# Router shares carried in the routed rows, and routed sums added by accumulating DMAs, in a two-layer kernel

## Chip, core and metric

The kernel runs on one core of a Trainium2 chip. The metric is the time of one execution on the device in microseconds. The core has TensorE (PE), VectorE (DVE), ScalarE (ACT), GpSimd (POOL) and SyncE (SP), each with an instruction stream of its own that runs strictly in order; they wait for each other by semaphores. SP issues plain DMAs, POOL the indirect ones (gathers and scatters by a list of row numbers).

## What is computed

Sixteen sequences of 256 tokens, 256 dimensions, go through two layers. The part that matters here is the mixture of experts of layer 0 and what layer 1 does first:

```python
x = x + tanh(g_xattn[0]) * retention(layernorm(x), ctx, ctx)
# router: 32 experts, the best 6 of a token, their scores normed to a sum of 2.5
topk_w = topk_w / (topk_w.sum(-1, keepdims=True) + 1e-20) * ROUTED_SCALE
h = relu2(einsum('th,eih->tei', x, up_w)) * combine[:, :, None]
moe_out = einsum('tei,ehi->th', h, down_w)
x = x + tanh(g_ffn[0]) * (moe_out + shared_expert(x))
# layer 1
x = x + tanh(g_xattn[1]) * softmax_attention(layernorm(x), ctx, ctx)   # 16 heads of 16
x = x + tanh(g_ffn[1]) * spiking_ffn(layernorm(x))
```

The share of an expert is a factor of its output row, so it may be applied wherever that row is at hand.

## The kernel before

The 16 sequences are eight groups of two (T = 512 tokens, four blocks `tt` of 128). Three stretches follow one another.

**Layer 0** (0 to about 511 us). Each engine has a list of steps with slot numbers; `turns` (L470) merges the steps of up to four groups into turns of 36 slots, older groups first within a slot. In it DVE works out for each group: the token's norm, the low half of the row (`low_row`, L835, a row is the token as two 16-bit halves, 1024 bytes), the router (`route_*`, up to L890), the rank of a token at its expert and so its row number (`rank`, `slot`, `slot_row`, L895 to L906), the shares (`weigh`, L911 to L925) and `add_shared` (L935). `weigh` stands at slot 97 of a group, that is slot 25 of a turn. It multiplies the chosen scores by their norm (`combine`, 128 x 4 x 32) and then picks the six shares of a token by comparing row numbers, in three operations of 128x768, into `share`, which stays in SBUF to layer 1. PE transposes the rows (L589) for the router and the shared expert. POOL sends each group's rows to the experts' places in HBM by 24 indirect DMAs (`xs<-w_hi,slot_row`, L1026), when the low halves and the row numbers are there.

**The routed experts** (about 518 to 755 us). 128 tiles of 256 rows in 64 pairs: SP loads a pair of `row_tile` (three buffers), PE transposes it, ACT and DVE copy, PE multiplies by the expert's first weights, ACT and DVE square the positive part, PE multiplies by the second, and two pairs later ACT (L1194) and DVE (L1246) each copy one tile of the output from PSUM, 128x512, to `y_tile`, which SP stores to `ys`. POOL does nothing here.

**Layer 1** (about 760 to 1578 us). Again steps by slots, in turns of 32 (`turns`, L1356), two sequences of 16 slots each to a group. Group g has its front in turn g (moments of x, `rstd`, `xn`, and the projections k, x, q, v by the slots of `FRONT`), its row maxima in the next (L1753), then the exponentials, and the tail (output projection, `power_f` at L1866, spiking network) in the two turns after that. The slots that matter here, in the turn of group g:

- slots 0, 2, 4, 6, 8, 10: DVE's `add_routed(k)` (L1707), four operations of 128x256 each: x_tok = share x y_in + x_tok
- slot 11: `moments_x`; slot 12: POOL's `power_x` (L1862); slot 15: `shift_x`
- slots 1 to 11.75: POOL's 24 gathers of group g+1 into `y_in` (L1856), each k behind the adds of k of group g, which free the buffer
- slots 19, 21, 23, 25: x0, x1, q0, q1 on PE
- slot 8: SP's load of x of group g+1 (L1379), which stands behind copies to `k_stack`
- slots 9 and 25: POOL's `power_f` for the tail of an older group's two sequences; DVE's `shift_f` (L1793) waits for it

The first group's 24 gathers stand ahead of the turns (L1883).

## Time and profile before

| | us |
|---|---|
| median of 3 runs | 1583.79 |
| lowest and highest | 1582.92, 1583.98 |
| the profiled execution | 1580.07 |
| its span from first to last instruction | 1578.3 |
| mean granted TensorE clock of it | 0.815 |

Differences are worked out in the profiled execution, between points of its span, and then set against its own time; that stands 3.7 us below the median, and this difference is added at the end. A row of the timeline gives the start, the duration and, in brackets, how long the engine sat idle before it and what ended that.

### The profile page before, as it was taken

To read this page: it belongs to the slowest core of one execution; us is meant where nothing else is said; L and a number is where in the kernel's file an instruction comes from. 1 tells how busy PE (TensorE), PEld (TensorE's weight loads), DVE (VectorE), ACT (ScalarE), POOL (GpSimd) and SP (SyncE) were. 2 spreads that over 40 slices of the span, in tenths; PEclk is the share of its full clock that TensorE was granted. 3 is DMA by queue.
4 is the path that set the end of the run, shared out by engine and by line. 5 is a ranking of instruction groups with operands and counts; after the bars stand their busy time and mean duration, and the time that the engine had idled before them with its cause. 6 is when DMAs were issued, how large, how long until landed. Compare 5 with 4: busy or idle time off the path is not lost.

```text
span 1578.3 us, 25639 instructions
## 1 busy us (share of the span) xinstructions
PE 1078.2 (68%) x8813; PEld 721.5 (46%) x8813; DVE 964.2 (61%) x2140; ACT 720.2 (46%) x1204; POOL 454.6 (29%) x444
## 2 busy tenths in 40 slices
PE   3766667766642799999204547586887778787875
PEld 1444434544321699899101214353545445454454
DVE  4574464665556477877615557577767767767433
ACT  2332232333343577777101336364646555655552
POOL 1134644653566000000564252406051510000000
PEclk9788878788766899999655659798988979888787
DMA  7513513321222798987534142414142321111100
GB/s 287 193 51 146 187 67 120 133 81 40 81 93 93 235 334 299 313 301 264 177 100 110 51 129 65 128 45 123 39 117 69 112 79 43 42 42 33 42 22 14
DMA packets 108140, 193.42 MB, mean 123 GB/s; under 512 B 21488, under 2 KB 46704, under 8 KB 107504
## 3 DMA queue, kind: packets, MB, share of 16 engines
q1 hardware_dynamic: 89584, 141.44, 27.0%
q0 software_dynamic: 18432, 50.36, 9.9%
q8 instruction: 75, 1.23, 0.3%
q14 instruction: 49, 0.40, 0.1%
HBM read 98.66 MB, written 79.95 MB: 113 GB/s over the span
## 4 chain that ended last, share of the span: by engine, by line
PE 21%; DVE 16%; issue 5%; another core or an unknown queue 4%; ACT 2%; DVEq 2%; DMA 1%; SPq 1%; ACTq 0%
PE bank L357 11%; DVE row_max L1753 5%; PE bank L1561 4%; PE bank L1517 3%; DVE x_tok L1707 3%; DVE spikes L1813 2%; PE bank L1477 2%; DVEq L1705 1%; PE bank L1500 1%; DVE mixed L1771 1%; DVE hid_lo L1804 1%; PE bank L383 1%; DVE spikes L1810 1%; DVE stats L1693 1%
## 5 line engine op out<-in xcount | busy, mean ns | idle before, releaser
L1753 DVE TENSOR_REDUCE row_max<-bank 128x2 f32<-128x512 f32 x256 | 164.9, 684 | 134.2 <-PE bank L1477 82.6
L1026 POOL DMA_INDIRECT xs<-w_hi,slot_row x192 | 196.7, 1024 | 117.6 <-DVE slot_row L906 62.1
L1856 POOL DMA_INDIRECT y_in<-ys,y_row x168 | 172.5, 1027 | 188.5 <-DVE x_tok L1707 141.1
L1625 ACT ACTIVATE prob<-bank 128x512 f32<-128x512 f32 x256 | 138.3, 589 | 90.5 <-PE bank L1500 58.4
L357 PE MATMUL bank<-xf_hi,w_hi 128*128 128x256 f16 (+1 forms) x320 | 114.3, 357 | 36.3 <-DVE xf_lo L1798 28.0
L1477 PE MATMUL bank<-k_stack,q_stack 48*128 48x256 f16 x512 | 58.4, 311 | 100.5 <-DVE row_max L1753 78.7
L357 PE MATMUL bank<-xf_hi,w_lo 128*128 128x256 f16 (+1 forms) x320 | 114.3, 357 | 2.3 <-issue 1.5
L357 PE MATMUL bank<-xf_lo,w_hi 128*128 128x256 f16 (+1 forms) x320 | 115.0, 359 | 1.1 <-issue 1.1
L1866 POOL TENSOR_TENSOR rstd_f<-var_eps_f,minus_half 128x2 f32<-128x2 f32 x16 | 15.0, 937 | 345.8 <-DVE var_eps_f L1698 345.7
L1883 POOL DMA_INDIRECT y_in<-ys,y_row x24 | 23.3, 972 | 256.4 <-issue 256.4
L357 PE MATMUL bank<-xt_tile,w_routed 128*128 128x256 f16 x768 | 95.2, 274 | 0.0
L1707 DVE SCALAR_TENSOR_TENSOR x_tok<-y_in,share,x_tok 128x256 f32<-128x256 f32 x192 | 80.5, 481 | 13.5 <-DMA y_in<-ys,y_row 8.4
L357 PE MATMUL bank<-w_routed,hid_tile_hi 128*128 x512 | 87.3, 273 | 0.8 <-DVE hid_tile_lo L1240 0.8
L357 PE MATMUL bank<-w_hi,ct 128*128 128x256 f16 x256 | 61.1, 323 | 37.6 <-DVE xt_lo L770 35.0
L357 PE MATMUL bank<-ct,w_hi 128*128 128x512 f16 x128 | 48.6, 459 | 54.2 <-DVE ct L794 30.2
L1477 PEld LDWEIGHTS bank<-k_stack,q_stack 48*128 48x128 f16 x512 | 16.4, 97 | 146.4 <-issue 74.6
L1517 PE MATMUL bank<-prob,v_one 128*32 128x256 f32 x1024 | 83.2, 447 | 0.0
L1173 ACT ACTIVATE xt_tile<-bank 128x1024 f16<-128x1024 f16 x64 | 65.5, 1023 | 33.4 <-PE bank L1126 33.4
L1126 PE MATMUL bank<-ident,row_tile 128*128 128x128 f16 x1024 | 69.3, 222 | 15.4 <-DMA row_tile<-xs 12.8
L1561 PE MATMUL bank<-w_hi,hid_hi 128*128 128x256 f16 x256 | 71.9, 281 | 10.0 <-DVE hid_lo L1804 7.1
L1236 DVE TENSOR_TENSOR hid_tile<-relu_tile 128x512 f32<-128x512 f32 x64 | 44.2, 691 | 55.4 <-ACT relu_tile L1183 55.4
L1500 PE MATMUL bank<-q_stack,k_stack 50*128 50x256 f16 x512 | 58.4, 307 | 27.8 <-ACT prob L1625 16.6
(214 smaller groups left out, 2799.8 us busy)
## 6 DMA issues: line engine op xcount, KB each, us to landing
row_tile<-xs SPq DMA_DIRECT2D x128, 256.0 KB, 3.6
ys<-y_tile SPq DMA_DIRECT2D x128, 256.0 KB, 3.4
xs<-zeros SPq DMA_DIRECT2D x32, 256.0 KB, 4.6
w_routed<-in_weights_r SPq DMA_DIRECT2D x4, 2048.0 KB
inverse<-den_mid SPq DMA_DIRECT2D x64, 128.0 KB
ctx_t<-in_ctx SPq DMA_DIRECT2D x8, 512.0 KB
ct_mid<-ct SPq DMA_DIRECT2D x8, 512.0 KB
ct<-ct_mid SPq DMA_DIRECT2D x8, 512.0 KB
```

The source lines that it names most:

```text
L357: mm = pe.matmul(dst, a, b, start=n == 0, stop=n == len(todo) - 1)
L1026: nc.gpsimd.indirect_dma_start(xs[:, :], bass.IndirectOffsetOnAxis(slot_row[p][:, tt, k:k + 1], axis=0), x_row[g % 3][:, tt, :, :].rearran ...
L1126: mm = pe.transpose(bank[:, c * TILE + h * P:c * TILE + (h + 1) * P], rows[n % NR][:, j, h, c * P:(c + 1) * P], ident16[:, :])
L1173: nc.scalar.activation(xt[n % NX][:, 0, :, :].rearrange("p c t -> p (c t)"), turn_bank[0][:, :].bitcast(F16), ACT.Copy).then_inc(rows_turn ...
L1477: mm = pe.matmul(firsts.bank((n, 2 * j + m))[:, qt * SEQ:(qt + 1) * SEQ], q_stack[n % NST][rows, j, qt * P:(qt + 1) * P], k_stack[n % NST] ...
L1500: mm = pe.matmul(seconds.bank((n, 2 * j + m))[:, kt * SEQ:(kt + 1) * SEQ], k_stack[n % NST][rows, j, kt * P:(kt + 1) * P], q_stack[n % NST ...
L1517: mm = pe.matmul(ubank[32 * c:32 * c + 32, half * SEQ:(half + 1) * SEQ], v_one[p][:, 2 * b + kt, BATCH * i + c, :], prob[:, (BATCH * i + c ...
L1561: mm = pe.matmul(acc[:, qt * D:(qt + 1) * D], a, b, start=(f, qt, k) == (0, 0, 0), stop=f == FC - 1 and k == 2, skip_group_check=True)
L1625: nc.scalar.activation(prob[:, h % NPR, :, :], seconds.bank((n, h))[:, :], ACT.Exp, scale=float(HD) ** -0.5).then_inc(seconds.reader((n, h ...
L1707: ins = V.scalar_tensor_tensor(out=x_tok[g % NXT][:, tt, :], in0=y_in[:, k, tt, :], scalar=share[:, g * TT + tt, k:k + 1], in1=x_tok[g % N ...
L1753: V.tensor_reduce(row_max[n % PAIR][:, :, m, j], firsts.bank((n, 2 * j + m))[:, :].rearrange("p (q k) -> p q k", q=2), AX_X, ALU.max).then ...
L1856: nc.gpsimd.indirect_dma_start(y_in[:, k, tt, :], None, ys[:, :], bass.IndirectOffsetOnAxis(y_row[:, g * TT + tt, k:k + 1], axis=0)) \
```

## The change

Three things are changed.

**Layer 0.** A row carries 32 float values more, the token's `combine` row (`ROW_COLS = D + EXPERTS`, 1152 bytes). `weigh` writes them straight into the row and ends there; the three 128x768 operations, `picked` and `share` are gone. It stands at slot 87 (slot 15 of a turn) and not 97, and POOL's sends wait for it too. The third row buffer has memory of its own, and `xs` and the zeros written to it have the new width.

**The routed experts.** Row tiles are 288 KB and not 256. POOL has a program now: for each pair it waits for the loaded tiles and copies the column of the tile's expert (number read from a third row of the table) into `row_share`, 128x2 for each tile (L1278 of the changed kernel). ACT and DVE scale the output by it, so that each copy is two of 128x256, and wait for it. SP loads into a buffer only when POOL has read it.

**Layer 1.** `y_in` and DVE's 24 adds of a group are gone. 24 indirect DMAs add the rows from `ys` straight to `x_tok`. For one `tt` each waits for the one before; the first waits for x of that group. They are issued at slots 2 to 13.5 of the turn before, behind `power_x`, which is at slot 1 now and not 12. `moments_x` is at slot 0 and waits for all 24. k1 goes from slot 7 to 6, x0 from 19 to 9, x1 from 21 to 11, q0 from 23 to 13, q1 from 25 to 15; k0, v0, v1 and the copies to the stacks (23 and 26) stay. The memset of `k_stack` is three over all partitions and not six of 32.

```diff
-    RANK_AT, SLOT_AT, WEIGH_AT, SEND_AT, X_OUT_AT = 88, 91, 97, 93, 99
+    RANK_AT, SLOT_AT, WEIGH_AT, SEND_AT, X_OUT_AT = 88, 91, 87, 93, 99
...
-                    V.tensor_tensor(combine[:, :, :], chosen[:, :, :],
-                                    total[:, :].unsqueeze(2).to_broadcast([P, TT, EXPERTS]), ALU.mult)
-                    done(V.tensor_tensor(picked[:, :, :, :],
-                                         slot[:, :, :].unsqueeze(2).to_broadcast([P, TT, TOP_K, EXPERTS]),
-                                         slot8[:, :, 0:TOP_K].unsqueeze(3).to_broadcast([P, TT, TOP_K, EXPERTS]),
-                                         ALU.is_equal))
-                    done(V.tensor_tensor(picked[:, :, :, :], picked[:, :, :, :],
-                                         combine[:, :, :].unsqueeze(2).to_broadcast([P, TT, TOP_K, EXPERTS]), ALU.mult))
-                    done(V.tensor_reduce(share[:, tts, :], picked[:, :, :, :], AX_X, ALU.add))
+                    V.tensor_tensor(x_share[g % 3], chosen[:, :, :],
+                                    total[:, :].unsqueeze(2).to_broadcast([P, TT, EXPERTS]), ALU.mult).then_inc(weighed.sem, 1)
...
+                        pool.wait_ge(weighed.sem, weighed.at(g, 0))
...
                         wait(sp, rows_full[1], n - NR + 1)
+                        wait(sp, shared_out, n - NR + 1)
...
-                        nc.scalar.activation(y[:, tile % NO, :, :].rearrange("p h d -> p (h d)"), y_bank[tile % NY][:, :],
-                                             ACT.Copy).then_inc(y_done[0], 1)
+                        act.wait_ge(shared_out, tile // 2 + 1)
+                        for h in range(2):
+                            ins = nc.scalar.activation(y[:, tile % NO, h, :], y_bank[tile % NY][:, h * D:(h + 1) * D], ACT.Copy,
+                                                       scale=row_share[:, tile // 2 % NS, 0, h:h + 1])
+                        ins.then_inc(y_done[0], 1)
...
+                    pool.wait_ge(rows_loaded[n % NR], 32 * (n // NR + 1))
+                    for j in range(2):
+                        wait(pool, y_done[j], n - NS + 1)
+                    for j in range(2):
+                        ins = nc.gpsimd.tensor_copy(row_share[:, n % NS, j, :].unsqueeze(2),
+                                                    rows[n % NR][:, j, :, bass.ds(expert_of[2 * n + j] + D, 1)])
+                    ins.then_inc(shared_out, 1)
...
-            MOE_AT = (0, 2, 4, 6, 8, 10)
-            NORM_X = 11
-            FRONT = {"k0": 4, "k1": 7, "x0": 19, "x1": 21, "q0": 23, "q1": 25, "v0": 27, "v1": 29}
+            NORM_X = 0
+            GATHER_AT = NORM_X + 2
+            FRONT = {"k0": 4, "k1": 6, "x0": 9, "x1": 11, "q0": 13, "q1": 15, "v0": 27, "v1": 29}
...
-                    dve.wait_ge(moe.sem, moe.at(g, TOP_K - 1))
+                    for s in y_added:
+                        dve.wait_ge(s, 16 * TOP_K * (g + 1))
...
+            def add_routed(pool, g, k, tt):
+
+                if k == 0:
+                    pool.wait_ge(x_in[g % NXT], 16 * (g // NXT + 1))
+                else:
+                    pool.wait_ge(y_added[tt], 16 * (TOP_K * g + k))
+                nc.gpsimd.indirect_dma_start(x_tok[g % NXT][:, tt, :], None, ys[:, :],
+                                             bass.IndirectOffsetOnAxis(y_row[:, g * TT + tt, k:k + 1], axis=0),
+                                             compute_op=ALU.add).then_inc(y_added[tt], 16)
...
-                    steps += [(MOE_AT[k] + 1 + tt / TT, gather, g + 1, k, tt) for k in range(TOP_K) for tt in range(TT)]
+                    steps += [(GATHER_AT + (TT * k + tt) / 2, add_routed, pool, g + 1, k, tt)
+                              for k in range(TOP_K) for tt in range(TT)]
```

On DVE in layer 0, in the middle of a turn, the kernel before has nothing of the router between the two output residuals (L825):

```order
L890 TENSOR_TENSOR before<-before,tally 128x32
L825 SCALAR_TENSOR_TENSOR w_lo<-bank,step_of,w_lo 128x512
L929 TENSOR_TENSOR hid_lo<-hid,hid_hi 128x512
L825 SCALAR_TENSOR_TENSOR w_lo<-bank,step_of,w_lo 128x512
L760 BN_STATS stats<-w_lo 128x6 x4
```

And later in the turn the weighing, `chosen` to `share`, ahead of the shared expert's addition (L935):

```order
L911 SCALAR_TENSOR_TENSOR chosen<-e_out,score 128x128
L913 TENSOR_REDUCE total<-chosen 128x4
L914 TENSOR_SCALAR total<-total 128x4
L915 RECIPROCAL total<-total 128x4
L916 TENSOR_SCALAR total<-total,step_of 128x4
L917 TENSOR_TENSOR combine<-chosen,total 128x128
L919 TENSOR_TENSOR picked<-slot 128x768
L923 TENSOR_TENSOR picked<-picked,combine 128x768
L925 TENSOR_REDUCE share<-picked 128x24
L935 SCALAR_TENSOR_TENSOR w_lo<-bank,step_of,w_lo 128x512 x2
L835 SCALAR_TENSOR_TENSOR w_hi<-xn,w_hi 128x4x256
```

And the changed kernel has it in the first of the two places:

```order
L829 SCALAR_TENSOR_TENSOR w_lo<-bank,step_of,w_lo 128x512
L926 TENSOR_TENSOR hid_lo<-hid,hid_hi 128x512
L915 SCALAR_TENSOR_TENSOR chosen<-e_out,score 128x128
L917 TENSOR_REDUCE total<-chosen 128x4
L918 TENSOR_SCALAR total<-total 128x4
L919 RECIPROCAL total<-total 128x4
L920 TENSOR_SCALAR total<-total,step_of 128x4
L921 TENSOR_TENSOR x_rows<-chosen,total 128x4x32
L829 SCALAR_TENSOR_TENSOR w_lo<-bank,step_of,w_lo 128x512
L764 BN_STATS stats<-w_lo 128x6 x4
L767 BN_AGGR moments<-stats 128x2 x4
L769 TENSOR_SCALAR var_eps<-moments 128x4
```

The weighing moved from just ahead of L935 and `low_row` (L835 before, L839 now) to between the residuals (L829 now).

On POOL in layer 1, one full turn in the middle, before (L1856 are gathers, L1862 `power_x`, L1866 `power_f`):

```order
L1862 TENSOR_TENSOR rstd<-var_eps,minus_half 128x4
L1866 TENSOR_TENSOR rstd_f<-var_eps_f,minus_half 128x2
L1856 DMA y_in<-ys,y_row 128x256 x16
L1866 TENSOR_TENSOR rstd_f<-var_eps_f,minus_half 128x2
L1856 DMA y_in<-ys,y_row 128x256 x8
L1862 TENSOR_TENSOR rstd<-var_eps,minus_half 128x4
```

and now (L1868 are the accumulating gathers, L1876 `power_x`, L1880 `power_f`):

```order
L1880 TENSOR_TENSOR rstd_f<-var_eps_f,minus_half 128x2
L1876 TENSOR_TENSOR rstd<-var_eps,minus_half 128x4
L1868 DMA x_tok<-ys,y_row 128x256 x13
L1880 TENSOR_TENSOR rstd_f<-var_eps_f,minus_half 128x2
L1868 DMA x_tok<-ys,y_row 128x256 x11
L1880 TENSOR_TENSOR rstd_f<-var_eps_f,minus_half 128x2
```

`power_x` stands ahead of the gathers and not behind them, and `power_f` behind 13 of them and not 16.

On DVE in layer 1, from the tail's `var_eps_f` to the end of the first half of a turn, before:

```order
L1698 TENSOR_SCALAR var_eps_f<-moments_f 128x2
L1707 SCALAR_TENSOR_TENSOR x_tok<-y_in,share,x_tok 128x256 x4
L1804 TENSOR_TENSOR hid_lo<-hid,hid_hi 128x512
L1753 TENSOR_REDUCE row_max<-bank 128x2 x2
L1731 TENSOR_TENSOR qk_lo<-qk,qk_hi 128x512
L1707 SCALAR_TENSOR_TENSOR x_tok<-y_in,share,x_tok 128x256 x4
L1810 TENSOR_SCALAR spikes<-bank 128x512
L1813 SCALAR_TENSOR_TENSOR spikes<-bank,spikes 128x512 x4
L1793 SCALAR_TENSOR_TENSOR shift_f<-moments_f,rstd_f 128x2
L1753 TENSOR_REDUCE row_max<-bank 128x2 x2
```

and now:

```order
L1723 TENSOR_SCALAR var_eps_f<-moments_f 128x2
L1745 TENSOR_TENSOR qk_lo<-qk,qk_hi 128x512
L1818 TENSOR_TENSOR hid_lo<-hid,hid_hi 128x512
L1767 TENSOR_REDUCE row_max<-bank 128x2 x2
L1739 SCALAR_TENSOR_TENSOR xt_lo<-bank,xt_hi 128x512
L1824 TENSOR_SCALAR spikes<-bank 128x512
L1827 SCALAR_TENSOR_TENSOR spikes<-bank,spikes 128x512 x4
L1807 SCALAR_TENSOR_TENSOR shift_f<-moments_f,rstd_f 128x2
L1767 TENSOR_REDUCE row_max<-bank 128x2 x2
```

The adds (L1707) are gone, and `xt_lo` of the front has come in.

## Rows read from the trace of the kernel before

**Rows 1.** The page's first part: busy time, share, instructions of each engine.
```profile
PE 1078.2 (68%) x8813; PEld 721.5 (46%) x8813; DVE 964.2 (61%) x2140; ACT 720.2 (46%) x1204; POOL 454.6 (29%) x444
```

**Rows 2.** Windows: us, busy time of each engine, PE clock, DMA share, GB/s.
```profile
600.00:650.00 50.00, 48.22 (x547) 44.03 (x545) 39.36 (x82) 37.40 (x57) 0.00 (x0) 1.00 0.94 320
700.00:750.00 50.00, 49.92 (x565) 45.78 (x562) 35.48 (x58) 36.74 (x56) 0.00 (x0) 1.00 0.78 270
850.00:900.00 50.00, 23.57 (x142) 9.69 (x142) 30.50 (x62) 12.84 (x23) 21.62 (x22) 0.60 0.32 87
```

**Rows 3.** Timeline of DVE in a turn of layer 0: start, duration, [idle before].
```profile
334.67 0.28 DVE L911 SCALAR_TENSOR_TENSOR chosen<-e_out,score 128x128 f32<-128x128 f32 x1
...
336.40 0.95 DVE L919 TENSOR_TENSOR picked<-slot 128x768 f32<-128x768 f32 x1
...
339.49 1.41 DVE L935 SCALAR_TENSOR_TENSOR w_lo<-bank,step_of,w_lo 128x512 f32<-128x512 f32 x2
```

**Rows 4.** Timeline of PE, two places of layer 0.
```profile
342.09 1.04 PE L589 MATMUL bank<-ident,w_hi 128*128 128x128 f16 x8 [6.56 <-DVE w_hi L835]
...
380.19 0.39 PE L357 MATMUL bank<-w_hi,ct 128*128 128x256 f16 x1 [5.44 <-DVE xt_lo L770]
```

**Rows 5.** Groups by line and form: busy, mean ns, idle before and releasers.
```profile
L357 PE MATMUL bank<-w_hi,ct 128*128 128x256 f16 x256 | 61.1, 323 | 37.6 <-DVE xt_lo L770 35.0 <-DVEq L1746 1.1 <-ACT qk L1591 1.0
...
L1194 ACT ACTIVATE y_tile<-bank 128x512 f32<-128x512 f32 x64 | 37.7, 588 | 1.5 <-PE bank L357 1.5
...
L1605 ACT ACTIVATE xn<-x_tok,shift,rstd 128x256 f32<-128x256 f32 x32 | 16.6, 589 | 62.1 <-issue 39.4 <-DVE shift L1720 22.7
...
L589 PE MATMUL bank<-ident,w_hi 128*128 128x128 f16 x128 | 13.2, 266 | 47.5 <-DVE w_hi L835 44.3 <-ACT w_hi L705 2.3 <-issue 0.9
...
L1739 DVE SCALAR_TENSOR_TENSOR v_one<-bank,bias_v 128x256 f32<-128x256 f32 x32 | 11.6, 405 | 6.8 <-PE bank L357 6.7
```

**Rows 6.** Timeline of ACT and DVE in one pair of the routed experts.
```profile
744.25 0.60 ACT L1183 ACTIVATE relu_tile<-bank 128x512 f32<-128x512 f32 x1 [0.73 <-PE bank L357]
...
744.88 0.69 DVE L1236 TENSOR_TENSOR hid_tile<-relu_tile 128x512 f32<-128x512 f32 x1 [1.02 <-ACT relu_tile L1183]
```

**Rows 7.** Timeline at the start of layer 1: SP, POOL and DVE.
```profile
760.02 0.43 SPq L1434 DMA_DIRECT2D x_tok<-x_mid  x1
...
790.10 0.95 POOL L1883 DMA_INDIRECT y_in<-ys,y_row  x1 [0.30 <-issue]
...
793.54 1.67 DVE L1707 SCALAR_TENSOR_TENSOR x_tok<-y_in,share,x_tok 128x256 f32<-128x256 f32 x4 [3.57 <-DMA y_in<-ys,y_row]
...
821.17 1.05 POOL L1862 TENSOR_TENSOR rstd<-var_eps,minus_half 128x4 f32<-128x4 f32 x1
...
845.87 1.28 DVE L1753 TENSOR_REDUCE row_max<-bank 128x2 f32<-128x512 f32 x2
```

**Rows 8.** The page's DMA part: issuer, count, KB each, us to landing.
```profile
row_tile<-xs SPq DMA_DIRECT2D x128, 256.0 KB, 3.6
```

**Rows 9.** Timeline of turn T5 of layer 1: DVE, SP and POOL.
```profile
1154.43 1.67 DVE L1707 SCALAR_TENSOR_TENSOR x_tok<-y_in,share,x_tok 128x256 f32<-128x256 f32 x4 [0.21 <-DVE max_lo L1759]
...
1165.37 0.59 SPq L1379 DMA_DIRECT2D x_tok<-x_mid  x1
...
1170.34 1.41 DVE L1753 TENSOR_REDUCE row_max<-bank 128x2 f32<-128x512 f32 x2 [4.71 <-remote]
...
1176.97 0.72 POOL L1866 TENSOR_TENSOR rstd_f<-var_eps_f,minus_half 128x2 f32<-128x2 f32 x1 [4.22 <-DVE var_eps_f L1698]
...
1176.97 1.67 DVE L1707 SCALAR_TENSOR_TENSOR x_tok<-y_in,share,x_tok 128x256 f32<-128x256 f32 x4
...
1186.40 0.15 DVE L1793 SCALAR_TENSOR_TENSOR shift_f<-moments_f,rstd_f 128x2 f32<-128x2 f32 x1
```

**Rows 10.** Chain of waits, 900 to 1320 us: start, duration, what; first and last of nine over 2.9 us.
```profile
907.67 8.15 another core or an unknown queue
...
1257.08 8.03 another core or an unknown queue
```

## What I expect of the change

> **What bounds the kernel now.** I read the busy shares first [rows 1]: no engine is busy for more than 68% of the span, so one number for the whole does not say what bounds it. The windows tell the stages apart [rows 2]: from 600 to 750 us, in the routed experts, PE is busy for 48 to 50 of 50 us at the full clock, and nothing but PE's work or the DMA queues can move that stage; from 850 to 900 us, in layer 1, PE works 23.6 us, DVE 30.5, ACT 12.8. Layer 0 and layer 1 are bound by chains that pass from engine to engine, and by the order in which each engine has its steps. So an instruction counts where the next engine waits for what stands behind it. In layer 0 that place is the stretch of DVE before `low_row` [rows 3], for which PE waits 6.56 us [rows 4], 44.3 us in all turns [rows 5]. In layer 1 it is the stretch between two row maxima, in which DVE adds the gathered rows [rows 9]; besides it, whole pieces of the chain of waits in which nothing that the trace knows is being waited for, nine of 2.9 us and more between 900 and 1265 us, 52.4 us together [rows 10]. They stand within a few us behind the load of x that SP issues in the middle of the 24 gathers (T5: issued 1165.37 us, DVE then idle; [rows 9, 10]), and none is left once the last load and the last gathers are through. I read them as something slow while the DMA queues are full; the trace doesn't name it. I count turns of layer 1 from 1, the one that starts at about 845 us; T5 starts at 1145.9 us.
>
> **Layer 0: three wide operations go, the weighing moves ten slots forward.** From `chosen` to the end of the third 128x768 operation is 334.67 to 339.49 us, 4.82 us that lie straight ahead of `add_shared` and `low_row`, without a gap on DVE [rows 3]. Of them 334.67 to 336.40, 1.73 us, remain as work (the six narrow operations; the last writes into the row in place of `combine`), and stand now between the two `residual` steps, ahead of `xt_lo`, for which PE waits 5.44 us at 380.19 [rows 4] and 35.0 us in all [rows 5]. DVE is busy without a gap there too, so these 1.73 us are on the path. PE's wait of 6.56 us is longer than the 4.82, so nothing else becomes late in front of it. Seven turns have both places: 7 x (-4.82 + 1.73) = -21.6 us. In the last group the weighing comes ahead of the ranks for which the last 24 sends wait: +1.7. The sum is **-20 us**. Ends: zero, if PE's other wait takes it all back, and -34, if the second place has cover. The sends carry an eighth more bytes at the same 1.02 us of POOL each, and the added wait of a send is for a step ten slots older than the low half of the row that it waits for already: nothing.
>
> **The routed stretch.** ACT's output copy of 588 ns becomes two of 128x256; the nearest rows are 589 ns for one of that shape (ACT, from SBUF) and, on DVE, 405 ns from PSUM [rows 5]. So between +0.2 and +0.6 us for each pair of tiles on ACT; with the 0.73 us that ACT sits idle before `relu` [rows 6] this is covered. DVE's copy, by its other 128x512 operation there 0.69 us [rows 6], becomes two of 405 ns: +0.12 us against 1.02 us of idle. POOL, idle until now, copies two 128x2 pieces for each pair; no row shows such a copy, its 128x4 power takes 1.05 us [rows 7], so about 2 to 3 us in 3.5 us a pair. It starts when the row tile has landed, and the output copies that want it come two pairs later. The three row buffers come free only after POOL as well, which works beside PE's transposes and is through before them. The DMA queues are nearer to their end: 1,049 KB a pair become 1,114, that is +6.25%, 317 GB/s from these two alone, some 340 with the weights that are loaded in the first part. By [rows 2] 320 GB/s is a share of 0.94 and 270 one of 0.78, so full would be 340 to 346. It fits, barely. I take **+1 us**, from 0 to +15 (6.25% of 237).
>
> The share and the rate of a window give some 345 GB/s at full. The Trainium skill (DMA: Bandwidth & Descriptors, "Where 436 GB/s comes from") has about 358 GB/s as a core's part of HBM, and 425 as measured by one core alone. This trace agrees with the lower one and speaks against the higher; by the higher the upper end of +15 would fall away and the sum stay.
>
> **Layer 1, what an accumulating gather costs.** POOL issues a gather every 1.25 us (0.95 busy, 0.30 between); one issued at 790.10 was used by DVE at 793.54, 3.4 us after its start, the longest of three seen [rows 7]. No row shows an accumulating one. Four of different `tt` are in the air and the fifth waits for the first, so a round of four takes max(5.0, L), with L the time from start to landing. Below, L can't be less than the 2.8 to 3.4 of a plain one, and the round stays at 5.0. Above, if all of L doubled because rows are read twice, it is 6.8. I take L = 5.3, nearer to the plain row since most of 3.4 us isn't transfer (128 KB at 345 GB/s is 0.4 us). A set of 24 is then 5 x 5.3 + 3.8 + 5.3 = 35.6 us until it has landed.
>
> The Trainium skill has a rule that speaks against this change (Collectives: The Full Stack, "The bandwidth ceiling: the fold count and why AG ≠ RS ≠ AR"): an add in the DMA path needs two source reads, and runs at half a copy's rate. No run here shows it yet. By it the transfer part doubles, 0.4 us more for each, which leaves the sum as it is.
>
> **The start of layer 1.** SP issues the load of x for group 0 at 760.02 [rows 7]; with 3.6 us for 256 KB [rows 8] and twice the bytes I put its landing at 765.5. Group 0's set has landed at 801.1 where before the last add ended at 795.2; but its `rstd` then comes at 803.5 and not at 821.17 [rows 7], since POOL no longer has group 1's 24 gathers ahead of it. The projections gain some 17 us. What is late next is group 1: its set starts behind `rstd`, at 804.5, has landed at 840.1, and its moments (2.3 us) stand at slot 0 of the next turn, on DVE ahead of the row maxima. So these start at 842.4 and not at 845.87: **-3.5 us**.
>
> **A turn of layer 1.** The 24 adds are six pieces of 1.67 us. In T5 four of them stand with no idle time around them (those at 1154.43 and 1176.97 in [rows 9] are two of the four), the other two before waits for PE or in a stall: -6.7 us a turn on the path, of 10.0. T1 has 30.5 us of DVE in 50 [rows 2], six tenths of 10: **-6**. T7 has adds and neither load nor gathers: **-6.7**. For T2 to T6: 5 x -6.7 = **-33.5**. The nine stalls: the load of x stays, but now nothing is gathered beside it, since the gathers wait for it, and then never more than four are in flight. Ends: 0 and all 52.4 us; I take a third, **-17.5**, since the load alone was issued into seven or eight queued gathers before.
>
> **What POOL's order takes back.** POOL now issues 13 gathers ahead of the odd sequence's `power_f` where it had 16, but they can't start before x has landed. In T5: the load was issued at 1165.37, behind `k_stack`; two of the four pieces are gone ahead of it, so 1162.0, landed 1167.1. The 13th gather starts three rounds later, at 1183.0, so `rstd_f` is there at 1185.2. Before it was there at 1177.7 and used at 1186.40 [rows 9], behind the spikes; without the adds DVE would want it at 1179.7. So DVE, and behind it row maxima for PE, waits 5.5 us: the first half of a turn gains 1.2 us and not 6.7. Behind it stand shorter things: the x and q projections that moved from slots 19 to 25 to slots 9 to 15 are done by PE and ACT in that wait, and their place in the second half is free. I count half as lost: 5 x 2.7 = **+13.7 us**; ends 0 and 27.5.
>
> **The sum.** -20 + 1 - 3.5 - 6 - 33.5 - 17.5 + 13.7 - 6.7 = -72.5 us. The profiled execution took 1580.07 us (1578.3 of span and 1.8 around it), 3.7 under the median of the runs shown: 1507.6 + 3.7 = **1511 us**. About 0.2% (3 us) is what can be told from no change.
>
> **Rivals.** *Slower: an accumulating gather takes long* (mechanism: the chain of six for a `tt`; place: POOL, behind which `power_f` waits, and the start of layer 1). Let the round be L. The start then gives +14.5 us at 6.8, +29 at 8, +53 at 10; each of T2 to T6 +3.3, +6.9, +12.9, since `rstd_f` is late by 3 L past 1169.3 against 1186.4, with nothing left of adds and stalls. With -20 + 1 - 6 - 6.7 from elsewhere: 6.8 gives -1 (1583), 8 gives +32 (1615), 10 gives +86 (1669). It decides from 6.8 us on. For it: no row, and the doubled reads. Against it: 3.4 us plain, of which 0.4 is bytes. Between 6.0 and 6.8 it gives 1545 to 1583.
> *Larger gain*: the stalls go whole (-35 more) and the half that I count as lost to POOL is all covered (-13.7): 1462; halfway 1486. For it: after 1260 us, without loads and gathers, there is none. Against: the load of x stays in each turn, and now meets accumulating traffic of the same turn right behind it.
> *The routed stretch becomes bound by DMA or POOL*: +15 in place of +1, 1525. For it: 0.94 of the queues were taken at 320 GB/s; against: the share falls to 0.78 once the weights are in.
> *The change doesn't do what it says in layer 0*: if PE's wait before `xt_lo` grows by what the other loses, the -20 are near 0: 1531.
>
> **How the numbers follow.** Forecast with its own terms (1486 to 1545, the third and fourth rival in it): 0.66. Larger gain (1462 to 1486): 0.13. L between 6.0 and 6.8 (1545 to 1583): 0.12, of which 0.04 are within 0.2%. L above: 0.09. Faster 0.66 + 0.13 + 0.08 = 0.87, same 0.04, slower 0.09. The range leaves out the lower half of the larger gain and the top: 1475 to 1560.
>
> **What would show it.** In the changed profile: PE's wait before the transposes of layer 0's rows falls from 44.3 us to some 12, the one before `xt_lo` matmuls rises from 35.0 by up to 12. The routed stretch has PE busy for 49 of 50 us and ACT's two copies under 0.6 us each. POOL's gathers of one `tt` stand 5.0 to 5.5 us apart; 6.8 or more proves me wrong. DVE's `shift_f` waits for `rstd_f` in each of T2 to T6 by 3 to 6 us. The unnamed pieces of the chain come to about 35 us; if they are gone, or double, my weakest term was wrong. The first row maximum is at 842 us less what layer 0 gained.

## The result and the profile after

| | before | changed |
|---|---|---|
| median, us | 1583.36 | 1614.73 |
| lowest and highest | 1568.95, 1583.98 | 1610.12, 1618.30 |
| the profiled execution; its span | 1580.07; 1578.3 | 1618.30; 1616.5 |
| ratio to before | | 1.023 (95%: 1.018 to 1.028) |

The change makes the kernel slower by 31 us; 1511 was forecast, faster by 72, with a range of 1475 to 1560. So both size and sign are wrong. Measured again on the chip of most of the experiments, the changed kernel was 1.021 of before (1.017 to 1.025).

The page of the changed kernel, busy time first, then three of its groups (line, what, count, then busy, mean ns, idle before):

```profile
PE 1077.3 (67%) x8815; PEld 725.7 (45%) x8815; DVE 869.4 (54%) x1986; ACT 729.1 (45%) x1268; POOL 592.1 (37%) x572
...
L1868 POOL DMA_INDIRECT x_tok<-ys,y_row x192 | 304.8, 1587 | 165.1 <-DMA x_tok<-x_mid 109.1
...
L1880 POOL TENSOR_TENSOR rstd_f<-var_eps_f,minus_half 128x2 f32<-128x2 f32 x16 | 18.4, 1148 | 230.3 <-DVE var_eps_f L1723 230.3
...
L1129 PE MATMUL bank<-ident,row_tile 128*128 128x128 f16 x1024 | 70.3, 223 | 24.7 <-DMA row_tile<-xs 18.7
```

A plain gather took POOL about 0.95 us [rows 7], an accumulating one takes 1587 ns in the mean, most of them 1545. POOL's line L1880, `power_f`, still waits for DVE; what it does to others is below. Two points on SP's queue cut the run in three, the first load of a row tile and the first load of x in layer 1:

```profile
539.40 1.92 SPq L1102 DMA_DIRECT2D row_tile<-xs  x4
...
787.88 0.43 SPq L1458 DMA_DIRECT2D x_tok<-x_mid  x1
```

Between start, these two points and the end of the span I get these stages; for before, the first row load is issued at 518.2 us, and the load of x in [rows 7] at 760.0.

| us | layer 0 | routed experts | layer 1 |
|---|---|---|---|
| before | 518.2 | 241.8 | 818.3 |
| changed | 539.4 | 248.5 | 828.6 |
| forecast of the difference | -20 | +1 | -54 |
| measured | +21.2 | +6.7 | +10.3 |

The three differences add up to 38 us and the medians differ by 31: the profiled execution of the changed kernel is the slowest of its four. The profile of before also has one short turn in layer 0 (below), so that stage differs by less against other executions.

**Layer 0.** The rows of the changed kernel that answer to [rows 3, 4], timeline of DVE, PE, ACT, POOL and PE again (start, duration, [idle before]):

```profile
350.55 1.41 DVE L932 SCALAR_TENSOR_TENSOR w_lo<-bank,step_of,w_lo 128x512 f32<-128x512 f32 x2
351.88 1.22 DVE L839 SCALAR_TENSOR_TENSOR x_rows<-xn,x_rows 128x1024 f16<-128x1024 f32 x1
...
355.54 0.19 PE L357 MATMUL bank<-w_hi,xf_lo 128*128 128x32 f16 x1
...
363.95 0.28 ACT L722 ACTIVATE expo<-bank 128x128 f32<-128x128 f32 x1 [8.17 <-remote]
...
363.15 0.97 POOL L1025 DMA_INDIRECT xs<-w_hi,slot_row  x1 [0.31 <-issue]
...
398.02 0.40 PE L357 MATMUL bank<-w_hi,ct 128*128 128x256 f16 x1 [6.83 <-DVE xt_lo L774]
```

DVE starts `add_shared` at 350.55 and `low_row` at 351.88, 5.3 us after that turn's row numbers (346.58, below) where it was 10.0 before: that half of the term came out as worked out. But the exponentials of the router (`expo`, L722), which want the logits of those rows, start at 363.95. The last of the 24 matmuls for the logits starts at 355.54. Before, the same two were these:

```profile
344.90 0.19 PE L357 MATMUL bank<-w_hi,xf_lo 128*128 128x32 f16 x1
...
347.57 0.28 ACT L718 ACTIVATE expo<-bank 128x128 f32<-128x128 f32 x1 [2.44 <-remote]
```

So what was 2.4 us is 8.2, and `expo` stands 17 us behind the row numbers in both (347.57 - 330.81 = 16.8; 363.95 - 346.58 = 17.4). The profile puts these waits to "remote", that is, it knows no event that ended them. By the program `expo` waits here for PE's logits, so I read it as the semaphore that PE raises coming long after the end that the record of its matmul gives. I had read that word only in layer 1. What happens in the same time is on POOL: it issues sends, one every 1.27 us. And at 398.02 PE waits 6.83 us for `xt_lo`, where it was 5.44.

`expo` is not the largest of these waits. In before's layer 0 ACT's `hid` (the hidden layer of the shared expert, L725) waits "remote" for 95.9 us in all, DVE's `sc` (L819) for 46.8 and `expo` for 20.4. The long ones end when the sends do. The last of that turn's sends in before, and the two waits that end behind it:

```profile
363.20 0.96 POOL L1026 DMA_INDIRECT xs<-w_hi,slot_row  x1 [0.30 <-issue]
364.78 0.56 DVE L819 TENSOR_TENSOR sc<-bank,table 128x384 f32<-128x384 f32 x1 [6.56 <-remote]
366.26 0.60 ACT L725 ACTIVATE hid<-bank 128x512 f32<-128x512 f32 x1 [14.61 <-remote]
```

A turn of layer 0 is so made of two parts: from the row numbers to the end of the last send, 330.81 to 364.2 = 33.3 us, and from there to the next row numbers, 23.8 us.

**Layer 1.** Turn T5, SP, POOL, DVE and PE; it answers to [rows 9]:

```profile
1206.97 0.59 SPq L1403 DMA_DIRECT2D x_tok<-x_mid  x1
...
1210.76 1.58 POOL L1868 DMA_INDIRECT x_tok<-ys,y_row  x1 [17.91 <-DMA x_tok<-x_mid]
...
1212.30 0.17 DVE L1723 TENSOR_SCALAR var_eps_f<-moments_f 128x2 f32<-128x2 f32 x1
...
1233.34 1.55 POOL L1868 DMA_INDIRECT x_tok<-ys,y_row  x1 [0.30 <-issue]
1234.33 1.32 POOL L1880 TENSOR_TENSOR rstd_f<-var_eps_f,minus_half 128x2 f32<-128x2 f32 x1
...
1235.68 0.16 DVE L1807 SCALAR_TENSOR_TENSOR shift_f<-moments_f,rstd_f 128x2 f32<-128x2 f32 x1 [16.05 <-POOL rstd_f L1880]
...
1237.19 0.61 PE L1501 MATMUL bank<-k_stack,q_stack 48*128 48x256 f16 x4 [19.45 <-DVE row_max L1767]
```

SP's load of x is issued at 1206.97 and has landed at 1210.76, on which POOL waited 17.91 us. The 13th gather is issued at 1233.34, that is 12 steps and 22.6 us later; `rstd_f` follows, and DVE's `shift_f` comes at 1235.68, after a wait of 16.05 us, and PE's next scores (L1501) after 19.45. The variance for it was ready at 1212.5. Over 900 to 1340 us, from the list of waits (who for whom: us in total, times, longest):

```profile
PE bank L1501 <- DVE row_max L1767: 124.2, 20, 20.0
...
POOL x_tok L1868 <- DMA x_tok<-x_mid: 87.4, 5, 19.8
DVE shift_f L1807 <- POOL rstd_f L1880: 82.1, 5, 17.6
```

No wait in this stretch is put to "remote", where the chain of before had nine unnamed pieces with 52.4 us [rows 10]. POOL at the start of layer 1, answering to [rows 7]: the first group's set and the `rstd` behind it,

```profile
793.32 1.63 POOL L1868 DMA_INDIRECT x_tok<-ys,y_row  x1 [21.72 <-DMA x_tok<-x_mid]
...
835.86 1.54 POOL L1868 DMA_INDIRECT x_tok<-ys,y_row  x1 [0.30 <-issue]
841.93 1.04 POOL L1876 TENSOR_TENSOR rstd<-var_eps,minus_half 128x4 f32<-128x4 f32 x1 [4.53 <-DVE var_eps L1723]
```

793.32 to 837.4 for 24 gathers, 44 us where 30 were seen before, and the second group's set is as long.

### The profile page after: what moved, and what is told of

Read it like the earlier page. It is cut to its first block, busy times and chain, and to the rows that moved or that the text cites. A ratio compares the mean times of both kernels' runs of the same rounds, so it can differ in the third digit from the quotient of the medians.

```text
span 1616.5 us, 25892 instructions
## 1 busy us (share of the span) xinstructions
PE 1077.3 (67%) x8815; PEld 725.7 (45%) x8815; DVE 869.4 (54%) x1986; ACT 729.1 (45%) x1268; POOL 592.1 (37%) x572
## 4 chain that ended last, share of the span: by engine, by line
PE 19%; POOL 14%; DVE 6%; issue 5%; ACT 3%; DMA 2%; SPq 1%; DVEq 1%; ACTq 0%; POOLq 0%
POOL x_tok L1868 14%; PE bank L357 9%; PE bank L1587 4%; PE bank L1543 3%; DVE spikes L1827 2%; DVE row_max L1767 1%; DMA x_tok<-x_mid 1%; PE bank L1501 1%; SPq L1414 1%; PE bank L1524 1%; ACT prob L1650 1%; DMA x_tok<-ys,y_row 1%; PE bank L1564 1%; ACT xn_f L1671 1%; ACT hid L1683 1%
## 5 line engine op out<-in xcount | busy, mean ns | idle before, releaser
L1868 POOL DMA_INDIRECT x_tok<-ys,y_row x192 | 304.8, 1587 | 165.1 <-DMA x_tok<-x_mid 109.1
L1025 POOL DMA_INDIRECT xs<-w_hi,slot_row x144 | 144.8, 1005 | 88.7 <-DVE slot_row L910 47.1
L1501 PE MATMUL bank<-k_stack,q_stack 48*128 48x256 f16 x512 | 56.7, 303 | 169.4 <-DVE row_max L1767 167.2
L357 PE MATMUL bank<-xf_hi,w_hi 128*128 128x256 f16 (+1 forms) x320 | 107.4, 336 | 32.3 <-DVE xf_lo L1812 21.7
L357 PE MATMUL bank<-xf_hi,w_lo 128*128 128x256 f16 (+1 forms) x320 | 107.6, 336 | 7.7 <-issue 7.7
L357 PE MATMUL bank<-xf_lo,w_hi 128*128 128x256 f16 (+1 forms) x320 | 107.9, 337 | 5.3 <-issue 5.3
L1501 PEld LDWEIGHTS bank<-k_stack,q_stack 48*128 48x128 f16 x512 | 16.1, 96 | 211.6 <-DVE row_max L1767 178.8
L1278 POOL COPY row_share<-row_tile 128x2 f32 x128 | 32.7, 286 | 206.4 <-DMA row_tile<-xs 182.7
L1880 POOL TENSOR_TENSOR rstd_f<-var_eps_f,minus_half 128x2 f32<-128x2 f32 x16 | 18.4, 1148 | 230.3 <-DVE var_eps_f L1723 230.3
L357 PE MATMUL bank<-w_hi,ct 128*128 128x256 f16 x256 | 66.8, 345 | 39.6 <-DVE xt_lo L774 37.8
L1671 ACT ACTIVATE xn_f<-x_tok,shift_f,rstd_f 128x256 f32<-128x256 f32 x32 | 17.6, 595 | 154.3 <-DVE shift_f L1807 154.3
L1129 PE MATMUL bank<-ident,row_tile 128*128 128x128 f16 x1024 | 70.3, 223 | 24.7 <-DMA row_tile<-xs 18.7
L729 ACT ACTIVATE hid<-bank 128x512 f32<-128x512 f32 x32 | 19.1, 596 | 139.6 <-remote 108.3
L568 PE MATMUL bank<-rot_q,rot_k 128*128 128x256 f32 (+1 forms) x256 | 59.4, 405 | 33.1 <-issue 31.6
L1176 ACT ACTIVATE xt_tile<-bank 128x1024 f16<-128x1024 f16 x64 | 65.8, 1029 | 33.8 <-PE bank L1129 33.8
L1129 PEld LDWEIGHTS bank<-ident,row_tile 128*128 128x128 f16 x1024 | 63.9, 100 | 29.1 <-DMA row_tile<-xs 22.0
```

Source lines behind the costliest of these rows:

```text
L357: mm = pe.matmul(dst, a, b, start=n == 0, stop=n == len(todo) - 1)
L568: mm = pe.matmul(bank[:, kt * SEQ:SEQ + kt * P], rot["k"][:, n % 2, keys], rot["q"][:, n, queries], start=n == 0, stop=n == 3)
L1025: nc.gpsimd.indirect_dma_start(xs[:, :], bass.IndirectOffsetOnAxis(slot_row[p][:, tt, k:k + 1], axis=0), x_whole[g % 3][:, tt, :], None) \
L1129: mm = pe.transpose(bank[:, c * TILE + h * P:c * TILE + (h + 1) * P], rows[n % NR][:, j, h, :].bitcast(F16)[:, c * P:(c + 1) * P], ident16 ...
L1176: nc.scalar.activation(xt[n % NX][:, 0, :, :].rearrange("p c t -> p (c t)"), turn_bank[0][:, :].bitcast(F16), ACT.Copy).then_inc(rows_turn ...
L1501: mm = pe.matmul(firsts.bank((n, 2 * j + m))[:, qt * SEQ:(qt + 1) * SEQ], q_stack[n % NST][rows, j, qt * P:(qt + 1) * P], k_stack[n % NST] ...
```

## The experiments

Two theories stood at the start, with their rivals in the expectations. A: layer 0 loses by its own edit, whatever layer 1 does (A1: by the weighing's new place). P: layer 1 loses because POOL issues its gathers, now dearer, only when x is there, and `power_f` stands behind them.

The experiments came to three chips. On two of them the kernel before takes about the same, 1573 and 1582 us on the one (e1 to e4, r1 to r4) and 1588 on the other (r5); on the third it takes 1447 (e5, e7, e8). I call them the slower chips and the faster chip. Every ratio is to the kernel before, measured beside it on the same chip. The stages are those of one execution each: of kernels that ran twice on the slower chips, layer 0 differs by 4 us (the changed kernel 539.4 and 543.2, e1 and r4 538.2 and 542.7).

| kernel | ratio (95%) | layer 0 | routed | layer 1 |
|---|---|---|---|---|
| e1, layer 1 as before | 1.012 (1.009 to 1.015) | 538.2 | 247.0 | 805.2 |
| e2, x early | 0.975 (0.972 to 0.978) | 540.6 | 245.1 | 752.4 |
| e3, plain gathers | 1.033 (1.029 to 1.037) | 538.7 | 246.0 | 844.2 |
| e4, before, no pick, weighing moved | 1.009 (1.005 to 1.012) | 536.0 | 242.0 | 805.2 |
| r1, the changed kernel | 1.021 (1.017 to 1.025) | 543.2 | 245.3 | 834.7 |
| r2, before, no pick | 0.999 (0.997 to 1.002) | 523.7 | 240.3 | 813.5 |
| r3, x early, weighing late | 0.967 (0.964 to 0.971) | 531.0 | 244.7 | 753.9 |
| r4 = e1 | 1.011 (1.008 to 1.015) | 542.7 | 243.9 | 804.5 |
| r5, more sends | 1.019 (1.013 to 1.024) | 618.0 | 245.8 | 755.2 |
| e5 = r2, faster chip | 0.999 (0.997 to 1.001) | 434.4 | 240.2 | 767.6 |
| e7 = r3, faster chip | 0.993 (0.990 to 0.995) | 436.7 | 245.0 | 748.0 |
| e8 = r5, faster chip | 1.035 (1.032 to 1.037) | 498.1 | 245.1 | 752.9 |

### Which stage: layer 1 undone (e1, r4)

```diff
-                                                     scalar=share[:, g * TT + tt, k:k + 1], in1=x_tok[g % NXT][:, tt, :],
+                                                     scalar=1.0, in1=x_tok[g % NXT][:, tt, :],
```

The part after layer 0 and the routed stretch is that of the kernel before; the diff shows its adds against those.

> The changed kernel in layer 0 and in the routed stretch, with the layer 1 of the kernel before (gathers into a buffer, 24 adds on DVE, old slots), its adds with a factor of 1 since the rows carry the shares; the arrivals of the fifth and sixth expert's rows share one semaphore. Theory A (layer 0 is slower because of its own edit): first row load at 539 us as in the changed kernel, routed stretch 247 us, layer 1 818 us: 1607. Theory B (layer 0 differs only by chance between executions): first row load at 515 to 520 us: 1585. In both layer 1 lasts 818 us again, 10 less than with the accumulating gathers.

> Layer 0 and the routed stretch changed, layer 1 with the plain gathers and DVE's adds of the kernel before. It was 1.012 of the kernel before where a turn takes 58 us. Theory: all of that is the weighing ahead of xt_lo (1.7 us in each turn) and the wider rows in the routed stretch (5 us), so it is the same amount of some 17 us on each chip: 1.012 to 1.015.

Measured: 1.2 and 1.1% slower, the first row load at 538.2 and 542.7 us. Theory A holds: layer 0 loses by its own edit; the six executions with it (538 to 543 us) stand 20 to 25 us behind the profile of before (518.2) and 15 to 20 behind r2 (523.7), which is as fast as before. Layer 1 took 805 us, not 818, and so the whole 1594 and not 1607: with the old layer 1 that stage takes 805 (e1, r4, e4) to 818 us (before), so the changed kernel's layer 1 (829, 835) loses some 10 to 30.

### The changed kernel again (r1)

> The changed kernel itself, to have it beside the others on one chip: the kernel before took 1573 to 1583 us on the chips of the first runs and 1447 on that of the last three, where a turn of layer 0 is 44 us and not 58 and no wait is put down to an unknown cause. Theory (POOL's order costs the same on each chip, 16 us in each of five turns, besides the longer sets at the start): 10 to 20 us slower than the kernel before in layer 1 here too. Where layer 0's turn is 58 us, a ratio of 1.02 to 1.03; where it is 44 us, 1.01 to 1.03.

Measured: 1620.0 us, 1.021; it ran on a slower chip, in the range for it. DVE's waits for `rstd_f` are there again, 65.8 us in four turns up to 1300 us.

### The load of x sooner (e2)

```diff
-                    steps += [(8, load_x, g + 1), (10, load_ctx, g + 1)]
+                    steps += [(0, load_x, g + 1), (10, load_ctx, g + 1)]
```

> The changed kernel with SP's load of x for the next group at slot 0 of a turn and not at slot 8. Theory P (POOL's order): the 13 gathers ahead of the odd power take 13 x 1.85 = 24 us on POOL and can start only when x has landed, 21 us after the start of a turn; DVE's shift_f waits 16 us for them in each of five turns. With x there 17 us sooner the wait is gone: 5 x 16 = 80 us less, some 1535 us. Rival Q (POOL's sum of work, 24 x 1.85 = 44 us a turn, or the DMA traffic is what costs): the wait turns up elsewhere, 1600 or more.

Measured: 1536.7 us, 0.975 of before, the layer 76 us shorter than the changed kernel's (81 between r1 and r3). The list of waits from 900 to 1340 us:

```profile
PE bank L1501 <- DVE row_max L1767: 55.6, 25, 7.3
POOL rstd_f L1880 <- DVE var_eps_f L1723: 53.7, 5, 20.7
```

DVE's wait for `rstd_f`, 82 us in the changed kernel, is 4.4 us here; POOL waits for the variance instead, that is, it is ready first. PE's wait for the row maxima is less than half. POOL has the same work in both (592 and 594 us busy), which speaks against rival Q. So theory P holds: the 16 us a turn were POOL's 13 gathers, started only when x was there. And layer 1 at 752 us is 53 to 66 us under that of before. My sum had -54 for it, but that this agrees is chance: the sum had +13.7 for POOL's order, which is gone here, only a third of the stalls, and a start that gains.

### Plain gathers in the same places (e3)

```diff
-                                             bass.IndirectOffsetOnAxis(y_row[:, g * TT + tt, k:k + 1], axis=0),
-                                             compute_op=ALU.add).then_inc(y_added[tt], 16)
+                                             bass.IndirectOffsetOnAxis(y_row[:, g * TT + tt, k:k + 1], axis=0)).then_inc(y_added[tt], 16)
```

> The changed kernel with plain gathers straight into x_tok, so the routed sums are left out of the result; chain of waits, slots and order are the same. Theory P: a gather costs POOL 0.95 + 0.30 = 1.25 us again and not 1.85, so 13 of them take 16 us and 24 take 30: the wait of shift_f falls from 16 to about 8 us, each set at the start is 14 us shorter: 5 x 8 + 2 x 14 = 68 us less, 1547 us. Rival R (the time is in the chain from landing to next issue, not in the instruction): gathers of one tt still stand over 7 us apart, no change.

This kernel leaves the routed sums out of its result. Measured: 1629 us, slower than the changed kernel, where 1547 was expected. The instruction is cheap again (groups by line: busy, mean ns, idle before):

```profile
L1868 POOL DMA_INDIRECT x_tok<-ys,y_row x192 | 184.2, 959 | 166.8 <-DMA x_tok<-x_mid 110.9 <-issue 56.0
```

so that part of theory P holds. DVE's wait for `rstd_f`, which was expected to halve, is gone, and the first row maximum of layer 1 comes 78.9 us after the first load of x where the changed kernel has 104.3 (2 x 14 us less were expected for the two sets). What the theory didn't have is the other side. The waits from 900 to 1340 us:

```profile
ACT prob L1650 <- remote: 49.3, 12, 12.7
...
DVE row_max L1767 <- remote: 29.2, 8, 14.9
...
DVE spikes L1824 <- remote: 26.7, 4, 8.9
```

The late results of PE are back, 105 us in these three lines, where the accumulating gathers had none. The expectation was missed by 82 us. The waits in the three lines lie partly beside each other on two engines, so they can't be added up against it; how much of the 82 us is theirs isn't shown. That the landing of a gather holds the next one of its `tt` is not it, since two of one `tt` stand 5.0 us apart, the bare pace of four issues.

### Layer 0: the three operations, and the place (e4, r2, e5)

```diff
-                    done(V.tensor_tensor(picked[:, :, :, :],
...
-                    done(V.tensor_reduce(share[:, tts, :], picked[:, :, :, :], AX_X, ALU.add))
```

In r2 and e5 that is all, the shares are a constant. e4 has also

```diff
-            RANK_AT, SLOT_AT, WEIGH_AT, SEND_AT, X_OUT_AT = 88, 91, 97, 93, 99
+            RANK_AT, SLOT_AT, WEIGH_AT, SEND_AT, X_OUT_AT = 88, 91, 87, 93, 99
```

> The kernel before without the three 128x768 operations of the weighing (the shares are a constant, so the routed part is weighed wrongly), and with the weighing at slot 87 and not 97; rows stay 1024 bytes, the sends don't wait for it. My prediction's term says -20 us: first row load at 498, 1563 in all. Theory A1 (the new place costs what the old one gave): first row load at 535 to 540 us, 1600. Theory A2 (the wider rows and the added wait cost it): first row load at about 500 us, 1565.

> The kernel before without the three 128x768 operations of the weighing and with the weighing where it was (slot 97); the shares are a constant, so the routed part is weighed wrongly. My prediction's term: 4.8 - 1.7 = 3 us for each of seven turns, that is -20 us or more. Theory S (while POOL issues the 24 sends, PE's results come late, and they come in full only when the last send is issued, so that what lies before this in a turn is covered by the sends): the three operations stood under the sends and cost nothing; first row load as in the kernel before, 518 to 525 us, total within 3 us of it.

> The kernel before without the three 128x768 operations, the weighing where it was; the shares are a constant. On the last chip it was 0.999 of the kernel before. Theory S says the same where a turn of layer 0 takes 58 us: within 3 us of the kernel before. My prediction's term says -20 us.

Measured: without the three operations 0.999 on both kinds of chip, so that removing the 3.1 us of DVE work in a turn (336.40 to 339.49 in [rows 3]) is worth nothing. With the weighing in its new place 1.009 (1.005 to 1.012), the first row load at 536 us, 12 later than without the move (r2): the place alone costs, theory A1. Two successive row numbers (`slot_row` on DVE) tell a turn of layer 0. The kernel before:

```profile
330.81 0.18 DVE L906 TENSOR_SCALAR slot_row<-slot 128x24 int32<-128x24 f32 x1
...
387.93 0.18 DVE L906 TENSOR_SCALAR slot_row<-slot 128x24 int32<-128x24 f32 x1
```

the changed kernel:

```profile
346.58 0.18 DVE L910 TENSOR_SCALAR slot_row<-slot 128x24 int32<-128x24 f32 x1
...
405.48 0.18 DVE L910 TENSOR_SCALAR slot_row<-slot 128x24 int32<-128x24 f32 x1
```

without the three operations (r2):

```profile
332.15 0.18 DVE L907 TENSOR_SCALAR slot_row<-slot 128x24 int32<-128x24 f32 x1
...
389.97 0.18 DVE L907 TENSOR_SCALAR slot_row<-slot 128x24 int32<-128x24 f32 x1
```

These turns are 57.1, 58.9 and 57.8 us; in r2 each of the first five is 57.8 or 57.9. Of before's first five four take 57.1 to 58.0 and one 52.7, so that some 5 of the 21 us are that one turn. PE's wait for `low_row`, by groups, in r2:

```profile
L590 PE MATMUL bank<-ident,w_hi 128*128 128x128 f16 x128 | 12.8, 260 | 26.2 <-DVE w_hi L836 22.2 <-ACT w_hi L706 3.1 <-issue 0.9
```

It is 22.2 us where before has 44.3 [rows 5]: half of it is gone, and the time is the same. The two parts of a turn say why (means of the first five turns, us):

| | row numbers to end of last send | from there to the next row numbers |
|---|---|---|
| before | 33.7 | 23.1 (four of 23.8 to 24.7, one of 18.2) |
| r2, no pick | 33.2 | 24.7 |
| e4, no pick, weighing moved | 33.2 | 26.1 |
| the changed kernel; r1 | 32.9; 33.1 | 26.6; 26.7 |
| r3, x early, weighing late | 32.9 | 24.6 |
| r5, more sends | 42.9 | 25.6 |

In the kernel before the weighing (334.67 to 339.49), `low_row` and PE's wait for it lie in the first part, beside the sends, and this part is as long with the three operations as without them. At its new place the weighing lies in the second part, ahead of `xt_lo`, and only this part grows, by 1.4 to 2.0 us over r2. The wider rows cost little: e1 and e4 differ by 2 us in layer 0.

### Both repairs together (e7, r3)

```diff
-            RANK_AT, SLOT_AT, WEIGH_AT, SEND_AT, X_OUT_AT = 88, 91, 87, 93, 99
+            RANK_AT, SLOT_AT, WEIGH_AT, SEND_AT, X_OUT_AT = 88, 91, 89, 93, 99
...
-                    steps += [(8, load_x, g + 1), (10, load_ctx, g + 1)]
+                    steps += [(0, load_x, g + 1), (10, load_ctx, g + 1)]
```

> The changed kernel with SP's load of x at slot 0 and with the weighing at slot 89, where DVE has it behind xt_lo and ahead of the ranks, in its wait of 5.7 us for PE, and not between the residuals. Theory S: this takes 1.7 us out of each of eight turns, the first row load comes at 525 to 528 us and not at 540, and the whole takes 1523 us against 1537 with the early load alone. Rival T (layer 0 is slower for its wider rows, not for the weighing's place): first row load at 540 again, 1537.

> The changed kernel with the early load of x and the weighing at slot 89. Theory: 80 us less than the changed kernel by the load, 12 by the weighing's place: ratio to the kernel before 0.965 where a turn of layer 0 takes 58 us, 0.993 where it takes 44 (as on the last chip).

Measured (r3): 1532.2 us, 0.967 of before, 88 less than the changed kernel beside it. DVE in one turn:

```profile
386.81 0.28 DVE L915 SCALAR_TENSOR_TENSOR chosen<-e_out,score 128x128 f32<-128x128 f32 x1
...
388.33 0.29 DVE L921 TENSOR_TENSOR x_rows<-chosen,total 128x128 f32<-128x128 f32 x1
392.69 0.29 DVE L899 SCALAR_TENSOR_TENSOR rank<-bank,mask 128x128 f32<-128x128 f32 x1 [4.07 <-PE bank L642]
```

The weighing runs from 386.81 to 388.6, and the ranks start when PE is done, after a wait of 4.07 us: it costs nothing here. Against r1, layer 0 gains 12 us and layer 1 81, as expected. It still stands 7 us behind r2 in layer 0; 6 of them are there already at the first row numbers (106.55 against 100.65 us), where two executions of one kernel differ by 3 (e1, r4), and no run shows what the rest is. On the faster chip the same kernel (e7) gains 0.7% (0.990 to 0.995). It is faster than both kernels on the slower chip, and than the kernel before on the faster. The times in us that were expected of e5, e7 and e8 were meant for the slower chips; r2, r3 and r5 answer them.

### More sends (e8, r5)

```diff
+                    if k < 2:
+                        nc.gpsimd.indirect_dma_start(spare[:, :], bass.IndirectOffsetOnAxis(slot_row[p][:, tt, k:k + 1], axis=0),
+                                                     x_whole[g % 3][:, tt, :], None) \
+                          .then_inc(sent[g % 3], 16)
```

> The kernel of the run before it (early load of x, weighing at slot 89) with 8 more sends in each group, of rows already sent, to a tensor that nothing reads: 32 sends and not 24. Theory S: a turn of layer 0 gets longer by the 8 issues of 1.27 us, 10.2 us, from 58 to 68 us, first row load at about 525 + 8 x 10 = 607 us. Rival: the sends have room in a turn (POOL is idle for some 27 of 58 us), a turn stays at 58 us and the first row load comes 10 us later at most, from the last group.

> Once more the 8 more sends of each group (32 and not 24), with the early load of x and the weighing at slot 89. On the chip where a turn of layer 0 took 44.5 us they made it 50.5, 6 of the 10.2 us that they take on POOL. Where a turn takes 57.7 us and PE's results come late for as long as POOL sends (theory S): 10 us more, 68 us, first row load at 531 + 80 = 611 us. Rival (PE's late results don't depend on the sends): 58 to 60 us, first row load by 541.

Measured on a slower chip (r5): each of the first five turns takes 68.3 to 68.8 us, the first row load is issued at 618.

```profile
381.62 0.18 DVE L910 TENSOR_SCALAR slot_row<-slot 128x24 int32<-128x24 f32 x1
...
449.94 0.18 DVE L910 TENSOR_SCALAR slot_row<-slot 128x24 int32<-128x24 f32 x1
```

Eight more sends of 1.27 us are 10.2, the turn grew by 11 against r3, which ran on the other slower chip (68.5 and 57.5 in the mean), 10 of them in the part with the sends. The long "remote" waits again end behind the last send:

```profile
423.38 0.97 POOL L1025 DMA_INDIRECT xs<-w_hi,slot_row  x1 [0.30 <-issue]
428.05 1.02 DVE L823 TENSOR_TENSOR sc<-bank,table 128x384 f32<-128x384 f32 x2 [12.79 <-remote]
428.28 0.60 ACT L729 ACTIVATE hid<-bank 128x512 f32<-128x512 f32 x1 [13.88 <-remote]
```

`expo` comes no later for it (21.0 us behind the row numbers at 381.62, 20.3 in r3 at 336.11); it is `hid` and `sc` that move with the end of the sends. So on the slower chips a turn of layer 0 is as long as its sends and what doesn't go beside them. That POOL itself holds the turn up behind its sends (its `rot_k`, the turned keys, stands there) is not it: POOL is idle for 8.66 us before it in before, waiting for DVE. On the faster chip (e8) the same edit added some 6 us to a turn, and 61 to the stage: the sends bound there too, but only in part. That chip has no late results of PE; the last logits and the exponentials of the kernel without the three operations there (e5):

```profile
294.58 0.19 PE L358 MATMUL bank<-w_hi,xf_lo 128*128 128x32 f16 x1
...
294.80 0.28 ACT L719 ACTIVATE expo<-bank 128x128 f32<-128x128 f32 x1
```

The logits end at 294.77 and `expo` starts at 294.80, where the slower chips had 2.4 to 4 us in before and 8.2 in the turn of the changed kernel above. The turn is 44 us there.

## Why the prediction was wrong

In the profiled pair the forecast is off by 41 us in layer 0, by 6 in the routed stretch and by 64 in layer 1. In the first a gain was counted that lay beside something longer; in the last the price of a gather on POOL was mis-sized, and with it the waits behind it.

**Layer 0, the term of -20.** The step that failed is "nothing else becomes late in front of it". The 4.82 us were there and went (PE's wait ahead of the transposes fell from 44.3 us to 4.2, where I gave 12), yet `expo` came no sooner. I took a wait of PE for DVE as proof that DVE was on the path. It lay under 33 us of sends: the waits for PE's results behind it (`expo`, then `hid` and `sc`) were "remote" in the same profile, and the last of them end 1 to 4 us behind the last send (r2: no gain; r5: the turn grows by what the sends grow). The other half of the term was right in sign and in size: the weighing ahead of `xt_lo` is on the path, and r3 against r1 gives 12 us for it, e4 against r2 12, and the turns alone 7 x 1.4 to 2.0 = 10 to 14, where I had 7 x 1.73 = 12.1. I counted it as the smaller part of a gain; it was the only part. Of the 21 us in the profiled pair, 5 more are one short turn of before; the other 4 stand already at the first row numbers (108.24 against 104.24 us), where two executions of one kernel differ by 3 (e1 105.61, r4 108.72). My fourth rival came nearest (layer 0 gives nothing), but it stopped at 0, and by its mechanism PE's wait for `xt_lo` had to grow by what the other loses; it grew from 35.0 to 37.8 us.

**The routed stretch.** +1 forecast, +6.7 measured in the profiled pair and +3.6 to +5.0 by r4, r3 and r1 against r2, in the range of 0 to +15. PE waited 18.7 us for row tiles where it had waited 12.8, and a 288 KB load took 4.5 us to land, not 3.6: it is the DMA side that got nearer, as said. "It fits, barely" came out, but my 340 to 346 GB/s for full queues were too low; the changed kernel from 580 to 620 us (the last two numbers are the share and GB/s):

```profile
580.00:620.00 40.00, 39.90 (x453) 36.58 (x451) 32.35 (x60) 33.16 (x58) 7.46 (x24) 1.00 0.97 351
```

POOL's copies are 286 ns, not the 1.05 us that I took from its power, and cost nothing that these traces show.

**What a gather costs.** I put all doubt into the landing, L, and took the 1.25 us between two issues as fixed. The chain never waited: gathers stand 1.84 us apart on POOL without a wait between, the busy time of the instruction itself grew from 0.95 to 1.54. A round of four takes 7.4 us and not 5.3. By my own rival that decides from 6.8 us on, 7.4 stands at 1599; it had the right place (POOL, with `power_f` behind), for the wrong reason. That its total lies near the 1615 measured is luck: it has +34.5 us in layer 1 and -19 before it, measured are +10 and +28. The rule that an add reads two sources (the Trainium skill, Collectives: The Full Stack, "The bandwidth ceiling: the fold count and why AG ≠ RS ≠ AR"), stated there for the reduce step of a collective, I had carried over to a gather and weighed in bytes alone, 0.4 us for each. POOL's DMA queue, on the pages of the changed kernel and of e3, shows the packets (packets, MB, share of 16 engines):

```profile
q0 software_dynamic: 36864, 53.50, 16.0%
...
q0 software_dynamic: 18432, 53.50, 10.0%
```

Both have 192 sends and 192 gathers, and 18,432 packets over 384 are 48 for each; that a send has 48 is borne out by r5, which has 64 more sends and 3072 more packets (39,936). So an accumulating gather has 144, three times a plain one's. The rule points the right way, though its two reads don't give the three times, and I did not ask whether the issuing instruction gets longer with them. That the 0.59 us more on POOL are for these packets is likely, not shown; shown is that both come and go with the add (e3).

**POOL's order.** The step was right: 13 gathers behind x, ahead of `power_f`, and DVE late. The size was 5.5 us a turn, half of it to be made good; measured 16.05 in T5, and PE stood for 19.45. 12 steps in 22.6 us against the 16 of three rounds of 5.3 is 6.6 of the 10.5 us; I have no row for the rest, and take it that the chain stands later in the turn. With x early the wait all but vanished (82.1 to 4.4 us), and layer 1 was 76 us shorter (e2): one slot number in SP's list.

**The stalls.** I had -17.5 of 52.4 us for them, the lowest-founded term. They went whole. What they were worth shows beside the faster chip, which has none of them: there layer 1 takes 768 us with the old gathers (e5) and 748 with the accumulating ones and x early (e7), 20 us less; on the slower chips the same two take 805 to 818 and 754 (r3). So the new layer 1 takes nearly the same on both kinds of chip, and 32 to 45 of its 51 to 64 us of gain stand only where results come late. The reason that I gave (full DMA queues behind the load of x) is not what the runs show: in e3 the load stands and the gathers are chained as in the changed kernel, and the stalls are there; in each of six profiles on the slower chips with plain gathers they stand in layer 1, and in none of the five with accumulating ones.

**The start of layer 1.** -3.5 forecast for the first row maximum; it comes 104.3 us after the first load of x, where before has 85.9: +18.5, from two sets of 44 us, not 35.6. By the first `max_lo`, some steps further on, it is +6 (129.9 and 124.0). (The set of the first group starts when x has landed, 5.4 us after its issue, as forecast.)

## What to carry to other kernels

A wait tells only who was late at that step; follow the work to the next step, and where that one waits "remote" or for no one, ask what holds it before counting an edit ahead of it as gain. Cut a turn at the points that move together over several kernels (here the row numbers and the last send) and see in which part the edited work lies. Price an unseen form of an instruction on the engine that issues it, not only by its landing, and multiply it by its place in the longest row behind which someone waits. When a chain is made to start behind an event, move that event forward in the same edit: here one slot number (8 to 0) turned 2% slower into 2.5% faster.

## What was not expected of the hardware

While POOL issues plain indirect DMAs beside PE's work, PE's results seem to come late on the slower chips: `expo` in layer 0 starts 2.2 to 9.0 us after the record of the last matmul it needs in before and the changed kernel, and up to 13.6 us after it in r1; DVE and ACT have waits of the same kind in layer 1, of up to 14.9 us (e3). They are not there with the accumulating gathers (none in layer 1 of the changed kernel, e2, r1, r3 and r5), and not at all on the faster chip, where the kernel before takes 1447 us and not 1580, with a turn of layer 0 of 44 us (e5) and not 58 (r2). What makes the chips differ, and whether PE works slower or only tells of its end late, the runs don't show.

An accumulating gather of 128 rows of 1 KB costs POOL 1.54 + 0.30 us, a plain one 0.95 + 0.30. A 128x2 copy on POOL took 0.29 us, its 128x4 power 1.04.
